# A convolution block on one core: thirteen slots instead of twelve, transfers by half slots, and four slots of one sample kept

## The chip, the cores and the metric

The kernel runs on one core of a Trainium2 chip. The time is the device time of one execution in microseconds (us). The kernel before takes 1641.06 us (median of three runs, 1640.28 to 1644.9).

## What is computed

x holds 16 samples of 64 x 64 pixels with 768 channels, in f32 (201.33 MB). Each sample is normalized in 32 groups of 24 channels, projected to 16 channels, and its mean decides the gates of four "experts": a 3 x 3 convolution after resizing by 1, 2, 4 and 8. The weighted sum is projected back to 768 channels and added to x.

```python
xc = conv2d(gn(x), conv1_w, conv1_b)                    # 768 -> 16, 1x1
pooled = mean(xc, (2, 3)); h = pooled @ H_w.T + H_b
g = softmax(where(top2(h), h, -inf))                    # 16 samples x 4 experts
experts = [down(conv2d(up(xc, 2**i), convl_w, convl_b)) for i in range(4)]
out = sum(stack(experts) * reshape(g, (4, 16, 1, 1, 1)))  # reshape, not transpose
return x + conv2d(out, conv2_w, conv2_b)                # 16 -> 768, 1x1
```

Because g is reshaped and not transposed, sample b is weighted with gates of the samples b//4, 4 + b//4, 8 + b//4 and 12 + b//4. So samples 0 to 3 need the means of samples 0, 4, 8 and 12; samples 4 to 7 those of 1, 5, 9 and 13; 8 to 11 those of 2, 6, 10 and 14; 12 to 15 those of 3, 7, 11 and 15.

## The kernel before, in words

A sample is 12.58 MB and on-chip memory holds twelve slots of 1.57 MB (128 partitions x 4 x 768 f32), an eighth of a sample each. Every sample passes twice. Stage A loads it (L), takes its statistics, transposes and projects it. Stage B comes after the gates of its quartet: it reloads the slots (R), adds the new values in place, and stores them (S). Only sample 15 is kept from A to B. So there are 128 loads, 120 reloads and 128 stores, 376 transfers of 1536 KB.

The order of work is written out in tables, one per engine, and each engine runs its table in order.

- SyncE runs TRANSFERS. `L4.3:3` loads slot 3 of sample 4 into place 3, `R0.4:1` reloads, `S0.0` stores, W1 and W2 are blocks of weight loads. A load waits until the place's former content has been transposed (stage A) or stored (stage B); a store waits for four adds. One transfer that waits holds all behind it.
- TensorE runs PE_ORDER: `T` transposes (24 a sample, L613), `M` projects (L626), `Z` sums the moments (L638), `G` and `H` do the gates (L657, L663), `C` is the convolution in seven parts (L678), `X` spreads the result (L695, L696), `E` projects back to 768 channels (32 tiles a sample, L707).
- ScalarE runs ACT_ORDER: `T` copies transposed data out of PSUM (L725), `S` takes 4 of 32 groups' statistics (L742, L744), `D` a square root, `I` and `H` copy results, `X` fills es4 (L778).
- VectorE runs DVE_ORDER: `B` is the statistics of 28 groups (L835), `F` turns them into scaled weights (L845 to L866), `V` and `W` prepare weights, `A` adds a tile to x in place (L915).
- GpSimd builds for each sample the weighted taps from four experts' tables (L560 to L564) and seven matrices "band" (L577), into BANDS = 4 buffers.

xT, the transposed data between ScalarE and TensorE, has XT = 4 buffers.

## Time and profile before

| what | value |
|---|---|
| median of the runs | 1641.06 us |
| the profiled execution | 1641.5 us |
| its span | 1639.8 us |
| PE, DVE, ACT, POOL busy | 1222.1, 1039.3, 657.6, 352.7 us |
| DMA moved | 593.46 MB, mean 362 GB/s |
| in the chain that ended last | DMA 45%, PE 28%, DVE 11%, SyncE's queue 7% |

The chain is followed back from the last instruction to what released each step. A transfer of 1536 KB takes long from issue to landing because several are queued; how far apart they follow one another is another number. Both can be read from the rows below.

### The profile page before, as it was taken

Reading aid. Unit: us, or ns where it says so; the run is one execution under the profiler, and the core shown is the slowest. Engines: PE = TensorE matmul, PEld = TensorE weight load, DVE = VectorE, ACT = ScalarE, POOL = GpSimd, SP = SyncE. Lnnn points to the kernel's source line nnn. Section 1 sums busy time; section 2 is a strip of 40 time slices with the busy share of each in tenths; the row PEclk is TensorE's granted clock in tenths of the full one; section 3 lists DMA queues with packets and bytes.
Section 4 is the critical chain, followed back from the end, with each engine's and each line's share of the span. In section 5 each row is a group of like instructions: output and inputs, shape, how many; then the busy total and the mean of one; then the engine's idle time right before and its main releaser. Section 6 shows DMA issues by size and latency. Waiting matters only on the chain.

```text
span 1639.8 us, 23721 instructions
## 1 busy us (share of the span) xinstructions
PE 1222.1 (75%) x8700; PEld 845.3 (52%) x8700; DVE 1039.3 (63%) x2763; ACT 657.6 (40%) x1549; POOL 352.7 (22%) x359
## 2 busy tenths in 40 slices
PE   1758879887889595949798968689597877766463
PEld 1636656655656363636565646366364544434231
DVE  7859765667576758555767575776845563453453
ACT  3758883444544453635454445435242100000000
POOL 2063008304010000052404100431004844211000
PEclk9889999989998797969889988799698887768555
DMA  9767774999999999957999999999999699999999
GB/s 359 270 230 273 280 298 157 397 350 406 367 406 397 409 398 409 393 222 289 400 343 392 379 408 378 406 335 410 410 402 403 237 403 411 415 413 415 414 414 381
DMA packets 203047, 593.46 MB, mean 362 GB/s; under 512 B 10290, under 2 KB 10290, under 8 KB 202932
## 3 DMA queue, kind: packets, MB, share of 16 engines
q1 hardware_dynamic: 202932, 591.95, 92.8%
q8 instruction: 69, 1.13, 0.3%
q14 instruction: 46, 0.38, 0.1%
HBM read 390.60 MB, written 201.33 MB: 361 GB/s over the span
## 4 chain that ended last, share of the span: by engine, by line
DMA 45%; PE 28%; DVE 11%; SPq 7%; issue 3%; ACT 2%; POOL 2%; DVEq 0%; ACTq 0%; POOLq 0%
DMA x_sb<-in_x 37%; PE ring_ps L613 11%; DMA out<-x_sb 8%; DVE x_sb L915 7%; PE img_ps L626 5%; SPq L427 5%; PE conv_ps L678 5%; PE ring_ps L707 5%; DVE stats L835 1%; POOL band L563 1%; PE ring_ps L695 1%; POOL taps L564 1%; ACT xT L725 1%; SPq L436 1%; PE ring_ps L638 1%
## 5 line engine op out<-in xcount | busy, mean ns | idle before, releaser
L915 DVE TENSOR_TENSOR x_sb<-x_sb,ring_ps 128x768 f32<-128x768 f32 x512 | 456.8, 949 | 358.1 <-PE ring_ps L707 188.4
L835 DVE BATCH_NORM_STATS2 stats<-x_sb 128x6 f32<-128x192 f32 x1792 | 472.5, 343 | 126.1 <-DMA x_sb<-in_x 68.5
L725 ACT COPY xT<-ring_ps 128x1024 f32<-128x1024 f32 x384 | 365.9, 1016 | 226.1 <-PE ring_ps L613 225.4
L613 PE MATMUL ring_ps<-ident,x_sb 128*128 128x128 f32 x3072 | 390.5, 285 | 72.7 <-DMA x_sb<-in_x 41.2
L707 PE MATMUL ring_ps<-w,es 128*128 128x512 f32 (+1 forms) x1024 | 322.6, 437 | 161.5 <-DVE x_sb L915 145.6
L613 PEld LDWEIGHTS ring_ps<-ident,x_sb 128*128 128x128 f32 x3072 | 354.5, 147 | 130.4 <-issue 88.6
L707 PEld LDWEIGHTS ring_ps<-w,es 128*128 128x128 f32 x1024 | 190.6, 229 | 275.2 <-DVE x_sb L915 152.3
L626 PE MATMUL img_ps<-xT,w 128*32 128x256 f32 x3072 | 219.9, 401 | 65.5 <-DVE w L866 55.0
L577 POOL TENSOR_TENSOR band<-taps,masks 128x640 f32<-128x640 f32 x112 | 169.7, 1541 | 444.0 <-PE conv_ps L678 442.8
L678 PE MATMUL conv_ps<-xc,band 128*128 128x1 f32 (+8 forms) x1120 | 219.9, 345 | 34.3 <-POOL band L577 20.5
L678 PEld LDWEIGHTS conv_ps<-xc,band 128*128 128x128 f32 x1120 | 156.1, 195 | 106.6 <-issue 93.4
L778 ACT CAST es<-ring_ps 64x1024 fp32r<-64x1024 f32 x64 | 63.5, 1004 | 363.5 <-PE ring_ps L696 363.3
L742 ACT ACTIVATE unread_squares<-x_sb 128x192 bf16<-128x192 f32 x256 | 93.6, 366 | 166.6 <-DMA x_sb<-in_x 127.8
L626 PEld LDWEIGHTS img_ps<-xT,w 128*32 128x32 f32 x3072 | 79.5, 111 | 149.1 <-DVE w L866 60.8
L560 POOL TENSOR_SCALAR taps<-experts,gates 128x400 f32<-128x400 f32 x16 | 20.6, 1285 | 590.7 <-DVE bias_es L900 585.7
L744 ACT ACTIVATE unread_copy<-x_sb 128x192 bf16<-128x192 f32 x256 | 89.7, 350 | 0.0
L695 PE MATMUL ring_ps<-es_hi,pick 128*64 128x512 f32 x128 | 64.2, 501 | 6.0 <-DVE bias_es L900 3.1
L563 POOL TENSOR_SCALAR band<-experts,gates 128x400 f32<-128x400 f32 x48 | 61.8, 1288 | 4.7
L696 PE MATMUL ring_ps<-es_lo,pick 128*64 128x512 f32 x128 | 61.2, 478 | 0.0
L638 PE MATMUL ring_ps<-stats,ones 128*128 128x192 f32 x128 | 35.1, 418 | 31.9 <-DVE stats L839 17.4
L564 POOL TENSOR_TENSOR taps<-taps,band 128x400 f32<-128x400 f32 x48 | 49.8, 1037 | 4.0
L742 ACT ACTIVATION_READ_ACCUMULATOR unread_squares<-x_sb 128x1 f32 x256 | 48.7, 190 | 0.0
(94 smaller groups left out, 341.8 us busy)
## 6 DMA issues: line engine op xcount, KB each, us to landing
x_sb<-in_x SPq DMA_DIRECT2D x248, 1536.0 KB, 18.5
out<-x_sb SPq DMA_DIRECT2D x128, 1536.0 KB, 12.9
w_rep<-in_L_conv_conv_w SPq DMA_DIRECT2D x8, 48.0 KB, 10.3
bias<-in_L_conv_conv_b SPq DMA_DIRECT2D x8, 0.1 KB, 10.0
wl_raw<-in_L_conv_convl_w SPq DMA_DIRECT2D x8, 9.0 KB, 7.0
bias_l<-in_L_conv_convl_b SPq DMA_DIRECT2D x8, 0.1 KB
gate_w<-in_L_conv_H_w SPq DMA_DIRECT2D x8, 0.2 KB
w_raw<-in_L_conv_conv_w SPq DMA_DIRECT2D x1, 48.0 KB
```

What stands on the lines that cost most here:

```text
L427: sp.dma_start(x_sb[:, n], x_v[s, i // 4, i % 4]).then_inc(loaded[n], 16)
L577: nc.gpsimd.tensor_tensor(band[:, n % BANDS], taps[:, MAT_ROW_TAP[m]].unsqueeze(2).broadcast_to(full), masks[:, MAT_MASK[m]].unsqueeze(1). ...
L613: last = nc.tensor.transpose(ring_ps[:, buf, q, half * P:(half + 1) * P], slot("L", a, 2 * c + half)[:, q, k * P:(k + 1) * P], ident[:, :])
L626: last = nc.tensor.matmul(img_ps[32 * q:32 * q + 32, 2 * P * (c % 2):2 * P * (c % 2 + 1)], w1[:, AI[a] % 2, k, c // 2, :], xT[:, at % XT, ...
L678: last = nc.tensor.matmul(conv_v[:, blk_out, col_out], band[:, n % BANDS, ax].rearrange("p h r -> p (h r)"), xc_v[:, XC_PLACE[b], blk_in, ...
L695: nc.tensor.matmul(into, high, es_hi[:, :], start=True, stop=False)
L707: last = nc.tensor.matmul(flat_ps[:, buf, part], es4[:, q, (i % 4) * P:(i % 4 + 1) * P], w2[:, part], start=True, stop=True)
L725: nc.scalar.copy(xT[:, at % XT], ring_ps[:, TURN["T", a, n] % RING]).then_inc(xT_copied, 1)
L742: nc.scalar.activation(unread_squares[:, :, :].rearrange("p (s q) c -> p s q c", s=2), group, ACT.Square, accum_out=stats[:, c, g, 0:1]).t ...
L744: nc.scalar.activation(unread_copy[:, :, :].rearrange("p (s q) c -> p s q c", s=2), group, ACT.Identity, scale=1.0 / HALF, accum_out=stats ...
L835: ins = nc.vector.bn_stats(stats[:, c, g, :], two_slots(n0, n1, g))
L915: nc.vector.tensor_tensor(x_sb[:, n, q, :], x_sb[:, n, q, :], flat_ps[:, TURN["E", b, t] % RING, 0:D], ALU.add).then_inc(added, 1)
```

## The change

Memory for a thirteenth slot comes from smaller buffers: XT goes from 4 to 3 and BANDS from 4 to 3; w1, pick, experts and masks shrink (expert 0 has only 3 x 3 taps that are not zero, and gets a table of its own; two of the five masks go, and the two matrices that used them are made by a memset and a product over one block). The spread (X) reads 32 of 128 rows of es_hi and es_lo.

Reloads and stores go by half slots of 768 KB, each half with its own semaphores; a half store waits for two adds. KEPT becomes {0: 4, 15: 8}: slots 0 to 3 of sample 0 stay on chip from A to B. There are 128 loads of 1536 KB, 232 reloads and 256 stores of 768 KB, 372 slots in all. The weights are loaded by ScalarE's queue, ahead of its first work. All four tables are written anew.

```diff
@@ -24,11 +24,11 @@
 CHUNKS = SPS // 2
 STEPS = CHUNKS * KB
 TILES = SPS * QN
-SLOTS = 12
+SLOTS = 13
 RING = 3
-XT = 4
+XT = 3
 XC = 6
-BANDS = 4
+BANDS = 3
 GV = G - 4
 HALF = 2 * QN * CG // 2
 GN_EPS = 1e-5
@@ -40,108 +40,138 @@
-KEPT = {15: 8}
+KEPT = {0: 4, 15: 8}
 TRANSFERS = """
-L4.0:0 L4.1:1 L4.2:2 W1 L4.3:3 L4.4:4 L4.5:5 L4.6:6 L4.7:7 L8.0:8 L8.1:9 L8.2:10 L8.3:11 L8.4:6 L8.5:7 L8.6:4 L8.7:5
+L4.0:0 L4.1:1 L4.2:2 L4.3:3 L4.4:4 L4.5:5 L4.6:6 L4.7:7 L8.0:8 L8.1:9 L8.2:10 L8.3:11 L8.4:12 L8.5:6 L8.6:7 L8.7:4
...
@@ -299,16 +341,17 @@
         x_sb = sb("x_sb", [P, SLOTS, QN, D])
         xT = sb("xT", [P, XT, QN, 2 * P])
         xc = sb("xc", [P, XC, PIX])
-        w1 = sb("w1", [P, 2, KB, 2, 2 * R])
+        w1 = sb("w1", [P, 2, KB, 3 * R])
         w1T = sb("w1T", [P, KB, R])
         stats = sb("stats", [P, CHUNKS, G, 6])
         ident = sb("ident", [P, P])
-        pick = sb("pick", [P, 2 * NH + 1, 2 * R], F32R)
+        pick = sb("pick", [P, 5, 2 * R], F32R)
         ones = sb("ones", [P, P])
         w2 = sb("w2", [P, D], F32R)
-        experts = sb("experts", [P, E, NT, NT, R])
+        experts = sb("experts", [P, E - 1, NT, NT, R])
+        expert_0 = sb("expert_0", [P, 3, 3, R])
         taps = sb("taps", [P, NT, NT, R])
-        masks = sb("masks", [P, 5, NH, R])
+        masks = sb("masks", [P, 3, NH, R])
         gates = sb("gates", [P, B, E])
         bias_es = sb("bias_es", [P, B])
         bias_l = sb("bias_l", [P, 1])
@@ -416,59 +459,42 @@
 
         @block.sync
         def _(sp):
-            def load(kind, s, i):
-                n, _, before = loads[kind, s, i]
-                if before is not None:
-                    was, s0, i0 = before
-                    if was == "L" and i0 >= KEPT.get(s0, 0):
-                        sp.wait_ge(transposed, AI[s0] * STEPS + (CHUNKS - i0 // 2) * KB)
+            stores = {half: 0 for half in stored}
+
+            def load(kind, s, i, place):
+                n, _, before = loads[(kind, s) + i]
+                for h, was in enumerate(before):
+                    if was is None:
+                        continue
+                    k0, s0, i0 = was[:3]
+                    half = (n[0], h) if kind == "L" else n
+                    if k0 == "L" and i0 >= KEPT.get(s0, 0):
+                        if h == 0:
+                            sp.wait_ge(transposed, AI[s0] * STEPS + (CHUNKS - i0 // 2) * KB)
                     else:
-                        sp.wait_ge(stored[n], 16 * stores[n])
-                sp.dma_start(x_sb[:, n], x_v[s, i // 4, i % 4]).then_inc(loaded[n], 16)
-
-            stores = [0] * SLOTS
-
-            def store(s, i):
-                kind = source[s, i]
-                n = loads[kind][0]
+                        sp.wait_ge(stored[half], 16 * stores[half])
+                if kind == "L":
+                    sp.dma_start(x_sb[:, n[0]], x_v[s, i[0] // 4, i[0] % 4]).then_inc(loaded[n], 16)
+                else:
+                    half = slice(2 * i[1], 2 * i[1] + 2)
+                    sp.dma_start(x_sb[:, n[0], 2 * n[1]:2 * n[1] + 2], x_v[s, i[0] // 4, i[0] % 4][:, half]
+                                 ).then_inc(loaded[n], 16)
+
+            def store(kind, s, i, place):
+                n = source[(s,) + i][1]
                 stores[n] += 1
-                sp.wait_ge(added, BI[s] * TILES + (i + 1) * QN)
-                sp.dma_start(out_v[s, i // 4, i % 4], x_sb[:, n]).then_inc(stored[n], 16)
-
...
+                sp.wait_ge(added, BI[s] * TILES + i[0] * QN + 2 * i[1] + 2)
+                sp.dma_start(out_v[s, i[0] // 4, i[0] % 4][:, 2 * i[1]:2 * i[1] + 2],
+                             x_sb[:, n[0], 2 * n[1]:2 * n[1] + 2]).then_inc(stored[n], 16)
+
+            for transfer in parse_transfers():
+                if transfer[0] == "S":
+                    store(*transfer)
                 else:
+                    load(*transfer)
+            for half in stored:
+                if stores[half]:
+                    sp.wait_ge(stored[half], 16 * stores[half])
@@ -554,14 +579,16 @@
 
                 flat = "p a x r -> p (a x r)"
                 all_e = taps[:, :, :, :].rearrange(flat)
-                for e in range(E):
-                    g, of_e = gates[:, b, e:e + 1], experts[:, e].rearrange(flat)
-                    if e == 0:
-                        link(nc.gpsimd.tensor_scalar(all_e, of_e, g, None, ALU.mult))
-                    else:
-                        part = band[:, NM * bi % BANDS].rearrange("p a h r -> p (a h r)")[:, 0:NT * NT * R]
-                        link(nc.gpsimd.tensor_scalar(part, of_e, g, None, ALU.mult))
-                        link(nc.gpsimd.tensor_tensor(all_e, all_e, part, ALU.add))
+                part = band[:, NM * bi % BANDS].rearrange("p a h r -> p (a h r)")
+                link(nc.gpsimd.tensor_scalar(all_e, experts[:, 0].rearrange(flat), gates[:, b, 1:2], None, ALU.mult))
+                for e in range(2, E):
+                    link(nc.gpsimd.tensor_scalar(part[:, 0:NT * NT * R], experts[:, e - 1].rearrange(flat),
+                                                 gates[:, b, e:e + 1], None, ALU.mult))
+                    link(nc.gpsimd.tensor_tensor(all_e, all_e, part[:, 0:NT * NT * R], ALU.add))
+                link(nc.gpsimd.tensor_scalar(part[:, 0:9 * R], expert_0[:, :, :, :].rearrange(flat), gates[:, b, 0:1],
+                                             None, ALU.mult))
+                link(nc.gpsimd.tensor_tensor(taps[:, 0:3, 0:3], taps[:, 0:3, 0:3],
+                                             part[:, 0:9 * R].rearrange("p (a x r) -> p a x r", a=3, x=3), ALU.add))
 
             for bi, b in enumerate(B_ORDER):
                 pool.wait_ge(gates_ready, b // 4 + 1)
@@ -573,9 +600,13 @@
                     n = NM * bi + part
                     if n >= BANDS and part:
                         pool.wait_ge(band_used, n - BANDS + 1)
-                    full = [P, NT, NH, R]
-                    nc.gpsimd.tensor_tensor(band[:, n % BANDS], taps[:, MAT_ROW_TAP[m]].unsqueeze(2).broadcast_to(full),
-                                            masks[:, MAT_MASK[m]].unsqueeze(1).broadcast_to(full),
+                    blocks = slice(0, 1) if m == TOP else slice(NH - 1, NH) if m == BOTTOM else slice(0, NH)
+                    if m in (TOP, BOTTOM):
+                        link(nc.gpsimd.memset(band[:, n % BANDS], 0.0))
+                    full = [P, NT, blocks.stop - blocks.start, R]
+                    nc.gpsimd.tensor_tensor(band[:, n % BANDS, :, blocks],
+                                            taps[:, MAT_ROW_TAP[m]].unsqueeze(2).broadcast_to(full),
+                                            masks[:, MAT_MASK[m], blocks].unsqueeze(1).broadcast_to(full),
                                             ALU.mult).then_inc(band_ready, 1)
 
         @block.tensor
@@ -690,10 +721,12 @@
                 for half in range(2):
                     h = 2 * (2 * (part % 2) + half) + part // 2
                     into = halves_ps[0:64, buf, half]
-                    high = pick[:, 2 * h + 1:2 * h + 3, :].rearrange("p n c -> p (n c)")
-                    low = pick[:, 2 * h:2 * h + 2, :].rearrange("p n c -> p (n c)")
-                    nc.tensor.matmul(into, high, es_hi[:, :], start=True, stop=False)
-                    last = nc.tensor.matmul(into, low, es_lo[:, :], start=False, stop=True)
+                    rows = slice(32 * (h // 2), 32 * (h // 2) + 32)
+                    first = 2 * (h % 2)
+                    high = pick[rows, first + 1:first + 3, :].rearrange("p n c -> p (n c)")
+                    low = pick[rows, first:first + 2, :].rearrange("p n c -> p (n c)")
+                    nc.tensor.matmul(into, high, es_hi[rows, :], start=True, stop=False)
+                    last = nc.tensor.matmul(into, low, es_lo[rows, :], start=False, stop=True)
                 last.then_inc(spread_done, 1)
 
             def tile(b, t):
@@ -715,6 +748,24 @@
 
         @block.scalar
         def _(act):
+            for h in range(NH):
+                rows = slice(R * h, R * h + R)
+                act.dma_start(w1_rep[rows, :], conv1_w.rearrange("r c y x -> r (c y x)")).then_inc(weights_in, 16)
+                act.dma_start(bias_1[rows, 0:1], conv1_b.unsqueeze(1)).then_inc(weights_in, 16)
...
+                act.dma_start(b2_raw[row:row + 1, :], conv2_b.unsqueeze(0)).then_inc(late_weights_in, 16)
             act.wait_ge(consts_ready, 1)
 
             def copy(a, n):
@@ -907,12 +959,12 @@
 
             def add(b, t):
                 i, q = divmod(t, QN)
-                kind = source[b, i]
-                n, count, _ = loads[kind]
-                if q == 0:
-                    dve.wait_ge(loaded[n], 16 * count)
+                load, (n, half) = source[b, i, q // 2]
+                place, count, _ = loads[load]
+                if q % 2 == 0:
+                    dve.wait_ge(loaded[place], 16 * count)
                 dve.wait_ge(expanded, BI[b] * TILES + t + 1)
-                nc.vector.tensor_tensor(x_sb[:, n, q, :], x_sb[:, n, q, :],
+                nc.vector.tensor_tensor(x_sb[:, n, 2 * half + q % 2, :], x_sb[:, n, 2 * half + q % 2, :],
                                         flat_ps[:, TURN["E", b, t] % RING, 0:D], ALU.add).then_inc(added, 1)
 
             program_of = {"B": groups, "F": fold, "L": low_half, "A": add, "P": softmax, "G": take_gates,
```

SyncE's queue at the start. Before: x_sb<-in_x are slots of x, the others are W1 and W2.

```order
1 L427 DMA x_sb<-in_x 128x4x768 x3
2 L441 DMA w_rep<-in_L_conv_conv_w 16x768
3 L442 DMA bias<-in_L_conv_conv_b 16x1
...
18 L427 DMA x_sb<-in_x 128x4x768 x13
19 L446 DMA wl_raw<-in_L_conv_convl_w 16x16x9 x8
20 L448 DMA w_raw<-in_L_conv_conv_w 128x6x16
...
38 L458 DMA b_raw<-in_L_conv_conv_b 1x768 x2
39 L427 DMA x_sb<-in_x 128x4x768 x32
40 L436 DMA out<-x_sb 128x4x768 x2
```

After:

```order
1 L477 DMA x_sb<-in_x 128x4x768 x41
2 L480 DMA x_sb<-in_x 128x2x768 x2
3 L477 DMA x_sb<-in_x 128x4x768 x3
4 L487 DMA out<-x_sb 128x2x768 x5
5 L480 DMA x_sb<-in_x 128x2x768
```

The 44 weight transfers are gone from SyncE's queue (they stand at the head of ScalarE's), and the first stores come after 45 slots' worth of loads, where 48 came before.

SyncE's queue between the last load of sample 5 and the first store of sample 5. Before, the third transfer of row 81 is L5.7, and row 90 begins with S5.0; 22 transfers lie from the one to the other, the store included.

```order
81 L427 DMA x_sb<-in_x 128x4x768 x5
82 L436 DMA out<-x_sb 128x4x768
83 L427 DMA x_sb<-in_x 128x4x768
84 L436 DMA out<-x_sb 128x4x768
85 L427 DMA x_sb<-in_x 128x4x768 x2
86 L436 DMA out<-x_sb 128x4x768
87 L427 DMA x_sb<-in_x 128x4x768 x2
88 L436 DMA out<-x_sb 128x4x768 x2
89 L427 DMA x_sb<-in_x 128x4x768 x9
90 L436 DMA out<-x_sb 128x4x768 x3
```

After, the last rows of the same stretch; it begins at row 89 (the first transfer there is L5.7), and row 121 begins with S5.0.0. From L5.7 to S5.0.0 it holds 27 slots' worth.

```order
109 L477 DMA x_sb<-in_x 128x4x768 x2
110 L487 DMA out<-x_sb 128x2x768
111 L477 DMA x_sb<-in_x 128x4x768
112 L487 DMA out<-x_sb 128x2x768
113 L480 DMA x_sb<-in_x 128x2x768
114 L477 DMA x_sb<-in_x 128x4x768
115 L487 DMA out<-x_sb 128x2x768
116 L480 DMA x_sb<-in_x 128x2x768 x2
117 L487 DMA out<-x_sb 128x2x768
118 L480 DMA x_sb<-in_x 128x2x768 x2
119 L487 DMA out<-x_sb 128x2x768 x2
120 L480 DMA x_sb<-in_x 128x2x768 x2
121 L487 DMA out<-x_sb 128x2x768 x3
```

Stores of sample 3 (rows 110 to 119) now stand right up to the first reloads and stores of sample 5, where nine loads in a row stood before. In the same way 33 transfers lay between L15.7 and S15.0 (the 256th and the 289th transfer), and 53.5 slots' worth lie there now (the 231st to the 284.5th).

GpSimd's work for one sample. Before, of 16 such blocks:

```order
183 L560 TENSOR_SCALAR taps<-experts,gates 128x400
184 L563 TENSOR_SCALAR band<-experts,gates 128x400
185 L564 TENSOR_TENSOR taps<-taps,band 128x400
186 L563 TENSOR_SCALAR band<-experts,gates 128x400
187 L564 TENSOR_TENSOR taps<-taps,band 128x400
188 L563 TENSOR_SCALAR band<-experts,gates 128x400
189 L564 TENSOR_TENSOR taps<-taps,band 128x400
190 L577 TENSOR_TENSOR band<-taps,masks 128x640 x7
```

After:

```order
259 L583 TENSOR_SCALAR taps<-experts,gates 128x400
260 L585 TENSOR_SCALAR band<-experts,gates 128x400
261 L587 TENSOR_TENSOR taps<-taps,band 128x400
262 L585 TENSOR_SCALAR band<-experts,gates 128x400
263 L587 TENSOR_TENSOR taps<-taps,band 128x400
264 L588 TENSOR_SCALAR band<-expert,gates 128x144
265 L590 TENSOR_TENSOR taps<-taps,band 128x3x48
266 L607 TENSOR_TENSOR band<-taps,masks 128x640 x5
267 L605 MEMSET band 128x640
268 L607 TENSOR_TENSOR band<-taps,masks 128x5x16
269 L605 MEMSET band 128x640
270 L607 TENSOR_TENSOR band<-taps,masks 128x5x16
```

One pair of passes over 400 elements is now over 144, and two of the seven products over 640 elements are a memset and a product over 80.

## Rows read from the trace of the kernel before

**Rows 1.** The page: DMA and GB/s over 40 slices, DMA queue, traffic of HBM.
```profile
DMA  9767774999999999957999999999999699999999
GB/s 359 270 230 273 280 298 157 397 350 406 367 406 397 409 398 409 393 222 289 400 343 392 379 408 378 406 335 410 410 402 403 237 403 411 415 413 415 414 414 381
q1 hardware_dynamic: 202932, 591.95, 92.8%
HBM read 390.60 MB, written 201.33 MB: 361 GB/s over the span
```

**Rows 2.** The DMA-issuing queue's waits: total us, times, longest.
```profile
SPq L436 <- DVE x_sb L915: 513.9, 121, 40.4
SPq L427 <- PE ring_ps L613: 300.7, 70, 23.4
SPq L427 <- DMA out<-x_sb: 178.1, 39, 14.9
```

**Rows 3.** Stretches: start:end, length, PE, PEld, DVE, ACT, POOL busy, clock, DMA, GB/s.
```profile
11.00:22.00 11.00, 1.51 (x6) 1.14 (x6) 7.66 (x30) 4.56 (x18) 0.00 (x0) 1.00 1.03 332
22.00:38.00 16.00, 0.28 (x2) 0.30 (x3) 15.97 (x64) 6.66 (x34) 0.00 (x0) 1.00 1.03 401
...
78.50:89.40 10.90, 10.90 (x117) 8.07 (x116) 7.61 (x29) 10.21 (x23) 0.00 (x0) 1.00 0.12 9
...
700.00:747.00 47.00, 28.69 (x164) 20.35 (x164) 25.27 (x96) 14.94 (x39) 31.45 (x24) 0.72 0.43 167
800.00:825.00 25.00, 16.37 (x85) 12.44 (x84) 16.23 (x52) 5.93 (x20) 14.75 (x12) 0.79 0.83 320
1070.00:1100.00 30.00, 22.84 (x164) 16.71 (x162) 23.76 (x44) 8.91 (x11) 13.02 (x10) 0.89 0.86 309
1267.00:1306.00 39.00, 32.55 (x167) 23.29 (x165) 18.21 (x22) 2.62 (x3) 29.78 (x23) 0.87 0.62 231
1330.00:1640.00 310.00, 185.62 (x613) 110.94 (x612) 145.06 (x164) 20.44 (x23) 50.17 (x37) 0.68 1.02 409
1628.00:1640.00 12.00, 0.00 (x0) 0.00 (x0) 0.00 (x0) 0.00 (x0) 0.00 (x0) 0.50 0.72 294
```

**Rows 4.** SyncE's issues at the start, in order of time: start us, us.
```profile
2.38 1.60 SPq L441 DMA_DIRECT2D w_rep<-in_L_conv_conv_w  x1
...
10.96 57.61 SPq L427 DMA_DIRECT2D x_sb<-in_x  x13
68.62 9.84 SPq L446 DMA_DIRECT2D wl_raw<-in_L_conv_convl_w  x8
...
89.45 188.09 SPq L427 DMA_DIRECT2D x_sb<-in_x  x32
280.81 3.84 SPq L436 DMA_DIRECT2D out<-x_sb  x2
```

**Rows 5.** VectorE in order of time at the start: start us, us.
```profile
21.94 7.37 DVE L835 BATCH_NORM_STATS2 stats<-x_sb 128x6 f32<-128x192 f32 x28 [3.06 <-DMA x_sb<-in_x]
...
49.94 0.35 DVE L852 RECIPROCAL norm<-norm 128x32 f32<-128x32 f32 x1 [2.12 <-ACT norm L729]
...
102.48 0.35 DVE L852 RECIPROCAL norm<-norm 128x32 f32<-128x32 f32 x1 [10.14 <-ACT norm L729]
...
114.36 0.96 DVE L814 CAST w_hi<-ring_ps 128x768 fp32r<-128x768 f32 x1 [2.96 <-PE ring_ps L651]
...
149.18 0.35 DVE L852 RECIPROCAL norm<-norm 128x32 f32<-128x32 f32 x1 [1.09 <-ACT norm L729]
192.32 0.35 DVE L852 RECIPROCAL norm<-norm 128x32 f32<-128x32 f32 x1 [0.85 <-ACT norm L729]
238.86 0.35 DVE L852 RECIPROCAL norm<-norm 128x32 f32<-128x32 f32 x1 [1.55 <-ACT norm L729]
```

**Rows 6.** SyncE's issues around the first store of sample 5.
```profile
612.40 19.56 SPq L427 DMA_DIRECT2D x_sb<-in_x  x5
...
672.58 34.38 SPq L427 DMA_DIRECT2D x_sb<-in_x  x9
747.34 7.29 SPq L436 DMA_DIRECT2D out<-x_sb  x3
```

**Rows 7.** SyncE's issues around the last samples' stores.
```profile
1126.89 26.74 SPq L427 DMA_DIRECT2D x_sb<-in_x  x7
...
1271.49 34.86 SPq L436 DMA_DIRECT2D out<-x_sb  x5
...
1507.24 10.92 SPq L427 DMA_DIRECT2D x_sb<-in_x  x3
...
1612.46 15.71 SPq L436 DMA_DIRECT2D out<-x_sb  x4
```

**Rows 8.** The page's DMA issues: KB each, us from issue to landing.
```profile
x_sb<-in_x SPq DMA_DIRECT2D x248, 1536.0 KB, 18.5
out<-x_sb SPq DMA_DIRECT2D x128, 1536.0 KB, 12.9
```

**Rows 9.** The page's groups of instructions that the smaller buffers touch.
```profile
L725 ACT COPY xT<-ring_ps 128x1024 f32<-128x1024 f32 x384 | 365.9, 1016 | 226.1 <-PE ring_ps L613 225.4
L577 POOL TENSOR_TENSOR band<-taps,masks 128x640 f32<-128x640 f32 x112 | 169.7, 1541 | 444.0 <-PE conv_ps L678 442.8
L678 PE MATMUL conv_ps<-xc,band 128*128 128x1 f32 (+8 forms) x1120 | 219.9, 345 | 34.3 <-POOL band L577 20.5
L563 POOL TENSOR_SCALAR band<-experts,gates 128x400 f32<-128x400 f32 x48 | 61.8, 1288 | 4.7
L564 POOL TENSOR_TENSOR taps<-taps,band 128x400 f32<-128x400 f32 x48 | 49.8, 1037 | 4.0
L695 PE MATMUL ring_ps<-es_hi,pick 128*64 128x512 f32 x128 | 64.2, 501 | 6.0 <-DVE bias_es L900 3.1
```

345 lines of the change are left out of this document (184 added, 161 removed).

## The prediction

> **What bounds the kernel now.** I read the page's slices first [rows 1]. All transfers go through one queue, its packets take 92.8% of sixteen engines' span, and in most slices the DMA digit is 9 with about 400 GB/s. The digits that are not 9 lie in two places: the first seven slices, where 157 to 298 GB/s are moved, and three dips, around slices 17 and 18, 26 and 31. So there are two regimes: near 400 GB/s only fewer bytes help, and in the holes something else is late. TensorE, busiest of the engines with 75% of the span, would leave 418 us, so it matters only where it stands in a chain.
>
> Next come the queue's waits [rows 2]: 513.9 us until VectorE's adds (stores), 300.7 until TensorE's transposes (loads of stage A), 178.1 until a store has landed (a place to become free). These are waits of the issuer, harmless while enough is queued: a load lands 18.5 us after its issue and a store 12.9 us [rows 8], while one slot at the 409 GB/s of 1330 to 1640 takes 1.573 MB / 409 = 3.85 us [rows 3]. About five slots are in flight. The stretches [rows 3] show where the cover is gone: 78.5 to 89.4 with 9 GB/s, 700 to 747 with 167, 1267 to 1306 with 231, and smaller ones at 800 (320) and 1070 (309).
>
> The first hole is explained by SyncE's own order [rows 4]. From 68.62 to 89.45 it issues the 28 transfers of W2, in 20.8 us, and the next load, of sample 12, is issued behind them. VectorE shows the price [rows 5]: its reciprocals of five samples stand at 49.94, 102.48, 149.18, 192.32 and 238.86, so periods of 52.5, 46.7, 43.1 and 46.5 us, and the long one contains a wait of 10.14 us for ScalarE's square root, which stands behind sample 12's statistics.
>
> The two large dips are the gates. S5.0 needs the gates of samples 1, 5, 9 and 13, thus all of A5. Its last load is the third of five issued from 612.40, the next stores of sample 5 come at 747.34, and after 672.58 nine loads end SyncE's work at 707 [rows 6]: every place is full and sample 3 is all stored. Similarly the last load of sample 15 is the fifth of seven issued from 1126.89, and after a wait five stores, among them the first of sample 15, take from 1271.49 to 1306.4 [rows 7].
>
> **The change, part by part.** The sum is made against the profiled execution, 1641.5 us (span 1639.8 and 1.7 around it), 0.4 above the median of 1641.06.
>
> *Weights on ScalarE's queue.* W1 goes from 2.38 to 10.96 on SyncE, with slot 4 of the first sample behind it, and VectorE waits 3.06 us for the second pair of slots [rows 4, 5]. Without W1, four slots at 409 GB/s are in at about 2 + 15.4 = 17.4 us, before VectorE is through with the first pair (18.9). So 3.1 us go. For W2, the wait of 10.14 goes, and of the next period (46.7 against 43.1, of which the wait of 2.96 for the weights' transposes is part, while VectorE's work on them stays) about 1: 11.1 us. The least is 0 (if another wait is just as late), the most 9.4 + 3.6 = 13. ScalarE now issues 44 transfers before its first statistics; at W1's pace (16 in 8.6 us) that is 23.6 us. It has sixteen groups to do before D4, four times half of the 6.66 us that two pairs of slots take in 22 to 38 [rows 3], and two copies (1016 ns [rows 9]), and would finish at 39, where VectorE's own part (four times 7.6 us from 11.2, and the weights' work) ends at about 43. This cover holds 4 us; beyond it each us counts fully.
>
> *GpSimd before the first store.* One of three added pairs of passes (1.288 + 1.037 us [rows 9]) is over 144 elements, not 400: if it goes by elements, 1.5 us, between nothing and 2.3. It is on the path once, before the first convolution. Later it is hidden behind other work. The first store waits for two adds instead of four, some 1.8 us, which I leave inside the other terms.
>
> *Slots kept and the thirteenth.* This is smaller than it looks. Four reloads vanish, 376 transfers become 372. But they vanish where the DMA had time: before the first store 48 loads were issued, now 45 slots' worth, as the kept slots occupy places. After it 328 were left (376 - 48), and now 327. One slot, 3.9 us.
>
> *Gates.* Here the thirteenth slot and the new tables count. Between L5.7 and S5.0 there were 22 transfers, 22 x 3.85 = 85 us, while the chain (statistics, projection, gates, matrices, convolution) took from a landing at about 640 to 747, 107 us. Now 27 slots' worth lie there, 104 us: 19 of the 26.8 us lost in 700 to 747 (0.57 of 47 [rows 3]) are covered. At sample 15 it is 33 against 53.5, which covers all of 0.38 x 39 = 14.8 us. The smaller holes at 800 and 1070 lose 4 us each, and I expect nothing there. Together 34 us at most; what was idle time of the DMA is no gain where the engines' own work is behind it, and it was at 70 to 83% for TensorE in these stretches. Nothing at all is the other end; nearer to the full cover, I take three quarters, 25 us.
>
> *Halves.* At the end the last store is half as long and waits for two adds: half a slot, 1.9 us, against a hole of 0.28 x 12 after 1628 = 3.4 us [rows 3]. There are 616 transfers instead of 376, 240 more. None of this size is in the trace. From above: in the stretch 11 to 22, where the 16 transfers of W1 pass in the queue, 332 GB/s were moved against 401 just after [rows 3]: 11 x (1 - 332/401) = 1.9 us, or 0.12 us each, so 29 us for 240. From below: nothing, and a gain is excluded since no byte is saved. Those weight transfers are of few and of tiny pieces, the halves of the same 3 KB pieces as before; I take 0.02 us, 5 in all, nearer to the row of the queue that is back-pressured at 10.92 us for three slots [rows 7], in which no gap can be seen.
>
> At this point a rule of the Trainium skill speaks against the change: "DMA: Bandwidth & Descriptors", on the anatomy of one DMA, gives a fixed cost of about 2.0 us per DMA (measured there for GpSimd's path) beside its bytes, most of it the wait for the last write to be confirmed. Were it paid one after another, the estimate by that page of the Trainium skill would be 240 x 2.0 = 480 us more. The row shows slots 3.6 us apart with 18.5 us from issue to landing, so by that rule, whose own account puts the cost into completion, the trace agrees: it lies in the latency and not in the spacing.
>
> *Smaller buffers.* ScalarE's copy takes 1016 ns and waits for TensorE, not the other way, in 225.4 us [rows 9]; with three buffers TensorE may transpose at most three ahead, and its tables do so. A band product takes 1541 ns, while a seventh of a convolution takes ten instructions, 219.9 us for 112 of them, so 1.96 us against 1.54. I cost both at nothing, hidden by DMA near 400 GB/s. If one band and one copy per sample came late it would be 16 x (1.54 + 1.02) = 41 us of TensorE; in the holes, a ninth of the span, that is 5 us. The cheaper last two of seven products can give back as much. The spread's matmuls (501 ns, 64.2 us in all) contract over 32 rows instead of 128: from nothing to half of that saved, off the path; I take nothing.
>
> Sum: 3.1 + 11.1 + 1.5 + 3.9 + 25 + 1.9 - 5 = 41.5, so 1600 us.
>
> **Rivals.**
>
> *Only the front and the bytes.* The dips stay since the rewritten tables put adds among stage A's work, and the same TensorE work has to be done before each gate. For it: TensorE is busy 0.83 of 1267 to 1306. Against it: only 0.61 of 700 to 747, where it waits for matrices and gates. Then 41.5 - 25 = 16.5, 1625 us.
>
> *DMA-bound from the first store on.* Between the 49th transfer at 280.8 and the 157th at 747.3, 4.32 us pass per transfer, and until the dip 3.96. If finer transfers and one more place bring all stretches to 3.85, 327 x 3.85 = 1259 us follow a first store at about 265, which is 1524; half of the way from 1600 to there is what I believe possible, since stage A is bound by its own work as at the start. About 1570 us.
>
> *The price of a transfer.* Each half costs the queue a fixed piece of time that cannot be overlapped. This is the mechanism on the other side: its place is every stretch near 400 GB/s, its price 240 times the piece, and from (41.5 + 5) / 240 = 0.19 us it makes the change slower than before. The row of W1 gives at most 0.12. At 0.12 it is 1600 + 24 = 1624, at 0.25 it is 1655. The Trainium skill's fixed cost per DMA ("DMA: Bandwidth & Descriptors", anatomy of one DMA) would be this mechanism if a tenth of it showed in the spacing.
>
> **How the numbers follow.** Forecast 1600 (its own range 1584 to 1616): 0.45. Front and bytes only, 1625: 0.23. DMA-bound, 1570: 0.17. Price of a transfer: 0.15, of which 0.10 above no change and 0.05 within it. No change is within 0.3% of 1641.06, thus 1636 to 1646. Of the second case 0.02 falls there. So faster 0.45 + 0.21 + 0.17 = 0.83, same 0.07, slower 0.10. The range of 1566 to 1636 leaves out most of the last case and a little of the third.
>
> **What would show it.** The gap of 10.14 us before a reciprocal gone and the first store near 265 (front). First store of sample 5 near 712 instead of 747 and over 300 GB/s before it; no stretch near 231 GB/s before the first stores of sample 8 (gates). 405 to 415 GB/s in the last 300 us with halves (price of a transfer: under 390 would make the third rival right). ScalarE's first statistics before 30 us. Wrong would be the forecast if the holes only moved, for instance to places where a half's wait holds SyncE's queue with less than five slots in flight.

## The result and the profile after

The changed kernel takes 1552.22 us (median of four runs, 1549.22 to 1555.05), the kernel before 1640.99 beside it: a ratio of 0.9454, interval 0.9431 to 0.9477. The gain is 88.8 us, where 41.5 were forecast. It lies outside the range, whose lower end was 1566. The profiled execution has a span of 1553.3 us.

The page's slices, main queue and traffic; they answer to [rows 1]:

```profile
DMA  9887845999999999999999999999999999999998
GB/s 327 315 305 275 304 155 199 411 409 395 380 410 410 410 409 390 410 345 394 407 408 409 397 400 362 411 415 415 415 415 413 383 405 413 414 412 410 415 413 333
q1 hardware_dynamic: 200320, 585.14, 96.0%
HBM read 384.30 MB, written 201.33 MB: 377 GB/s over the span
```

The first seven slices are still below 330 GB/s. Of the three dips one is left, shallower, at slice 17 (345; the first slice is 0, as in the prediction). Outside it 407 to 415 is what most slices show, where before 335 to 400 came up again and again. The queue's waits (total us, times, longest), against [rows 2]:

```profile
SPq L487 <- DVE x_sb L967: 291.7, 152, 6.4
SPq L477 <- PE ring_ps L644: 251.7, 67, 20.7
SPq L480 <- DMA out<-x_sb: 171.5, 68, 9.2
SPq L480 <- PE ring_ps L644: 38.2, 3, 35.3
```

Waiting for adds fell from 513.9 to 291.7 us, waiting for transposes only from 300.7 to 289.9 (251.7 in loads and 38.2 in reloads, one of these 35.3 long). Store waits have a longest of 6.4 us, where before one lasted 40.4.

To see where the 86.5 us between the two spans lie, I cut both executions at the same events: the first stores of samples 0, 3, 5, 4, 10 and 8, found by counting SyncE's issues against its list. Stretches of the kernel before (columns as in [rows 3], GB/s last):

```profile
280.80:585.40 304.60, 246.35 (x1883) 172.03 (x1884) 210.94 (x573) 142.16 (x339) 43.74 (x33) 0.89 1.00 390
585.40:747.30 161.90, 116.43 (x948) 82.17 (x945) 100.19 (x319) 79.78 (x191) 31.75 (x25) 0.84 0.85 332
747.30:1070.40 323.10, 264.56 (x1999) 187.06 (x2000) 218.73 (x622) 155.13 (x377) 64.24 (x48) 0.89 0.99 386
1070.40:1163.20 92.80, 75.10 (x575) 53.17 (x575) 65.08 (x151) 39.77 (x89) 17.18 (x13) 0.91 0.98 375
1163.20:1334.40 171.20, 141.03 (x839) 95.08 (x837) 101.60 (x165) 40.01 (x52) 67.49 (x51) 0.88 0.93 364
1334.40:1639.80 305.40, 181.71 (x590) 107.94 (x590) 141.28 (x160) 20.35 (x22) 45.93 (x34) 0.68 1.02 409
```

and of the changed one:

```profile
263.20:569.70 306.50, 256.92 (x2070) 180.18 (x2074) 228.94 (x656) 166.46 (x400) 41.22 (x40) 0.91 1.02 404
569.70:695.40 125.70, 97.01 (x759) 67.81 (x748) 92.63 (x288) 65.30 (x162) 27.16 (x26) 0.85 0.99 386
695.40:1027.10 331.70, 295.41 (x2434) 210.73 (x2434) 249.94 (x731) 192.68 (x454) 67.82 (x65) 0.94 1.02 398
1027.10:1087.50 60.40, 55.89 (x418) 38.88 (x419) 31.59 (x52) 22.69 (x25) 4.10 (x4) 0.89 1.03 415
1087.50:1245.90 158.40, 124.24 (x566) 78.67 (x564) 94.09 (x122) 19.50 (x23) 59.08 (x58) 0.78 1.02 407
1245.90:1553.30 307.40, 186.52 (x588) 104.98 (x586) 142.60 (x159) 20.41 (x22) 41.78 (x41) 0.60 1.00 402
```

In its best slices the kernel before moved 414 GB/s or so; at that rate a slot of 1.573 MB takes 3.80 us. What each stretch takes beyond 3.80 us for each of its slots I call its excess:

| from first store of | slots before, after | excess before, us | excess after, us | gained, us |
|---|---|---|---|---|
| start, to sample 0 | | 280.8 in all | 263.2 in all | 17.6 |
| 0 to 3 | 75, 79.5 | 19.6 | 4.4 | 15.2 |
| 3 to 5 (first gate) | 33, 28.5 | 36.6 | 17.4 | 19.2 |
| 5 to 4 | 80, 86 | 19.1 | 4.9 | 14.2 |
| 4 to 10 | 23, 16 | 5.4 | -0.4 | 5.8 |
| 10 to 8 (second gate) | 41, 41 | 15.4 | 2.6 | 12.8 |
| 8 to the end | 76, 76 | 16.6 | 18.6 | -2.0 |

With the one slot fewer (3.8) this is 86.6. So 17.6 us come at the front, 32.0 at the two gates, and 35.2 in the three stretches between, where the DMA digit was 9 before too. I call those the mixed stretches: stage A of one sample runs beside stage B of another.

How full the queue was there can be read from the same traces, by cutting them into pieces of 4 us and counting what was issued and had not landed. In the mixed stretches before, fewer than two slots were in flight for 84 us, and these pieces moved 290 GB/s; measured by bytes they hold 25 of 48 us of excess. With three slots or more in flight it was 401 GB/s for 533 us (17 us of excess), where the end of the kernel has 413. After, the pieces with fewer than two slots are 32 us at 343 GB/s (5.5 of 20 us), and with three or more it is 407 GB/s. So some 20 of the 28 us that this count shows as gained are time in which the queue had run short.

The first store of sample 5, against [rows 6] (start us, us):

```profile
682.85 4.19 SPq L487 DMA_DIRECT2D out<-x_sb  x2
688.50 2.22 SPq L480 DMA_DIRECT2D x_sb<-in_x  x2
695.37 3.83 SPq L487 DMA_DIRECT2D out<-x_sb  x3
```

It comes at 695.37 instead of 747.34, and SyncE issues reloads until 4.7 us ahead of it, where before it issued nothing for 40 us. ScalarE at the start:

```profile
9.10 8.47 ACTq L756 DMA_DIRECT2D wl_raw<-in_L_conv_convl_w  x8
...
18.11 9.33 ACTq L760 DMA_DIRECT2D gate_b<-in_L_conv_H_b  x1
...
35.40 0.79 ACTq L768 DMA_DIRECT2D b_raw<-in_L_conv_conv_b  x2
36.30 1.28 ACT L793 ACT_TABLE_LOAD   x1 [36.30 <-issue]
```

Its 44 weight transfers last until 36.2 us, and its first statistics follow at 36.30, where the prediction wanted them before 30. VectorE's first two pairs of slots, and the first step after its statistics of the first sample, which waits for TensorE's sums:

```profile
14.65 7.37 DVE L888 BATCH_NORM_STATS2 stats<-x_sb 128x6 f32<-128x192 f32 x28 [10.16 <-DMA x_sb<-in_x]
...
23.42 7.37 DVE L888 BATCH_NORM_STATS2 stats<-x_sb 128x6 f32<-128x192 f32 x28 [1.13 <-DMA x_sb<-in_x]
...
53.87 0.36 DVE L898 TENSOR_REDUCE small<-ring_ps 128x96 f32<-128x192 f32 x1 [4.48 <-PE ring_ps L669]
```

The same in the kernel before (its second pair is in [rows 5], at 21.94):

```profile
11.24 7.37 DVE L835 BATCH_NORM_STATS2 stats<-x_sb 128x6 f32<-128x192 f32 x28 [6.96 <-DMA x_sb<-in_x]
...
46.69 0.36 DVE L845 TENSOR_REDUCE small<-ring_ps 128x96 f32<-128x192 f32 x1 [0.69 <-PE ring_ps L638]
```

The first pair of slots is there 3.4 us later than before and the second 1.5 us later. VectorE's reciprocals of the first five samples, against [rows 5]:

```profile
56.86 0.35 DVE L905 RECIPROCAL norm<-norm 128x32 f32<-128x32 f32 x1 [1.76 <-ACT norm L780]
...
97.88 0.35 DVE L905 RECIPROCAL norm<-norm 128x32 f32<-128x32 f32 x1 [1.09 <-ACT norm L780]
...
141.97 0.35 DVE L905 RECIPROCAL norm<-norm 128x32 f32<-128x32 f32 x1 [1.09 <-ACT norm L780]
...
182.94 0.35 DVE L905 RECIPROCAL norm<-norm 128x32 f32<-128x32 f32 x1 [1.09 <-ACT norm L780]
...
223.21 0.35 DVE L905 RECIPROCAL norm<-norm 128x32 f32<-128x32 f32 x1 [0.40 <-ACT norm L780]
```

The first is 6.9 us later than before (49.94), the others 4.6, 7.2, 9.4 and 15.7 earlier. The wait of 10.14 is gone. The page's issues, against [rows 8], show that a half lands 14.4 us after its issue:

```profile
x_sb<-in_x SPq DMA_DIRECT2D x128, 1536.0 KB, 16.0
out<-x_sb SPq DMA_DIRECT2D x256, 768.0 KB, 14.4
x_sb<-in_x SPq DMA_DIRECT2D x232, 768.0 KB, 14.4
```

### The profile page after: what moved, and what is told of

Read it like the earlier page. It is cut to its first block, busy times and chain, and to the rows that moved or that the text cites. A ratio compares the mean times of both kernels' runs of the same rounds, so it can differ in the third digit from the quotient of the medians.

```text
span 1553.3 us, 24104 instructions
## 1 busy us (share of the span) xinstructions
PE 1208.5 (78%) x8700; PEld 827.1 (53%) x8700; DVE 1030.2 (66%) x2747; ACT 665.3 (43%) x1549; POOL 312.2 (20%) x381
## 4 chain that ended last, share of the span: by engine, by line
DMA 45%; PE 30%; SPq 9%; DVE 8%; ACT 2%; ACTq 2%; issue 2%; POOL 1%; DVEq 0%
DMA x_sb<-in_x 32%; PE ring_ps L644 13%; DMA out<-x_sb 13%; PE img_ps L657 6%; PE conv_ps L709 6%; DVE x_sb L967 5%; SPq L480 5%; SPq L487 4%; PE ring_ps L740 3%; DVE stats L888 1%; ACT unread_squares L793 1%; ACT unread_copy L795 1%; ACTq L760 1%; ACTq L756 1%; SPq L477 1%
## 5 line engine op out<-in xcount | busy, mean ns | idle before, releaser
L776 ACT COPY xT<-ring_ps 128x1024 f32<-128x1024 f32 x384 | 375.8, 1014 | 263.5 <-PE ring_ps L644 233.2
L644 PE MATMUL ring_ps<-ident,x_sb 128*128 128x128 f32 x3072 | 401.1, 289 | 65.0 <-DMA x_sb<-in_x 41.3
L740 PE MATMUL ring_ps<-w,es 128*128 128x512 f32 (+1 forms) x1024 | 337.5, 446 | 145.2 <-DVE x_sb L967 140.4
L644 PEld LDWEIGHTS ring_ps<-ident,x_sb 128*128 128x128 f32 x3072 | 361.1, 149 | 128.6 <-issue 97.2
L709 PE MATMUL conv_ps<-xc,band 128*128 128x1 f32 (+8 forms) x1120 | 227.5, 351 | 19.2 <-POOL band L607 10.3
L607 POOL TENSOR_TENSOR band<-taps,masks 128x640 f32<-128x640 f32 (+1 forms) x112 | 133.0, 1202 | 530.9 <-PE conv_ps L709 527.1
L793 ACT ACTIVATION_READ_ACCUMULATOR unread_squares<-x_sb 128x1 f32 x256 | 48.7, 190 | 0.0
L795 ACT ACTIVATION_READ_ACCUMULATOR unread_copy<-x_sb 128x1 f32 x256 | 48.5, 189 | 0.0
L728 PE MATMUL ring_ps<-es_hi,pick 32*64 32x512 f32 x128 | 33.1, 530 | 13.4 <-DVE x_sb L967 12.0
L585 POOL TENSOR_SCALAR band<-experts,gates 128x400 f32<-128x400 f32 x32 | 41.2, 1286 | 3.1
L669 PEld LDWEIGHTS ring_ps<-stats,ones 128*128 128x128 f32 x128 | 23.5, 218 | 31.8 <-DVE stats L892 23.3
## 6 DMA issues: line engine op xcount, KB each, us to landing
out<-x_sb SPq DMA_DIRECT2D x256, 768.0 KB, 14.4
x_sb<-in_x SPq DMA_DIRECT2D x232, 768.0 KB, 14.4
```

Source lines behind the costliest of these rows:

```text
L607: nc.gpsimd.tensor_tensor(band[:, n % BANDS, :, blocks], taps[:, MAT_ROW_TAP[m]].unsqueeze(2).broadcast_to(full), masks[:, MAT_MASK[m], bl ...
L644: last = nc.tensor.transpose(ring_ps[:, buf, q, half * P:(half + 1) * P], slot("L", a, 2 * c + half)[:, q, k * P:(k + 1) * P], ident[:, :])
L709: last = nc.tensor.matmul(conv_v[:, blk_out, col_out], band[:, n % BANDS, ax].rearrange("p h r -> p (h r)"), xc_v[:, XC_PLACE[b], blk_in, ...
L740: last = nc.tensor.matmul(flat_ps[:, buf, part], es4[:, q, (i % 4) * P:(i % 4 + 1) * P], w2[:, part], start=True, stop=True)
L776: nc.scalar.copy(xT[:, at % XT], ring_ps[:, TURN["T", a, n] % RING]).then_inc(xT_copied, 1)
L793: nc.scalar.activation(unread_squares[:, :, :].rearrange("p (s q) c -> p s q c", s=2), group, ACT.Square, accum_out=stats[:, c, g, 0:1]).t ...
```

## The experiments

All ratios are against the kernel before on the same chip.

### The changed kernel with one part undone

**Whole transfers, same orders.** The two words of a half pair are merged where the second stood.

```diff
-L2.4:11 S0.5.0 S0.5.1 L2.5:2 S0.6.0 S0.6.1 L2.6:3 R0.7.0:8.0 R0.7.1:8.1 L2.7:6 R1.0.0:0.0 R1.0.1:0.1 L3.0:4 S0.7.0
+R0.5:12 S0.3 R0.6:10 S0.4 L2.4:11 S0.5 L2.5:2 S0.6 L2.6:3 R0.7:8 L2.7:6 R1.0:0 L3.0:4 L3.1:12 S0.7 L3.2:10 S1.0 R1.1:8
...
-                sp.wait_ge(added, BI[s] * TILES + i[0] * QN + 2 * i[1] + 2)
+                sp.wait_ge(added, BI[s] * TILES + (i[0] + 1) * QN)
```

> The changed kernel with reloads and stores of whole slots (1536 KB), each at the place in SyncE's order where its second half stood, everything else as changed. Theory 1 (the 63 us of holes went because of the thirteenth place and the new order; halves only shorten the tail): 1555 to 1565 us. Rival (halves did it: a place turns over sooner since half a store and half a reload can start after two adds): 1585 to 1615 us, with holes at the gates and less than 400 GB/s between 330 and 1000 us.

Measured: 1719.88 us, 1.0485 (1.0466 to 1.0505), 168 us above the changed kernel. The queue's waits:

```profile
SPq L455 <- DVE x_sb L934: 697.7, 121, 24.0
SPq L449 <- PE ring_ps L611: 483.9, 73, 32.4
```

The waits for adds went from 291.7 to 697.7 us. This is far above both expectations (1555 to 1565 and 1585 to 1615): the order cannot do without halves as it stands; whether another list of transfers would let it is tried below.

**Weights back on SyncE's queue**, W1 behind the third load and W2 behind L8.7 as before.

```diff
-L4.0:0 L4.1:1 L4.2:2 L4.3:3 L4.4:4 L4.5:5 L4.6:6 L4.7:7 L8.0:8 L8.1:9 L8.2:10 L8.3:11 L8.4:12 L8.5:6 L8.6:7 L8.7:4
+L4.0:0 L4.1:1 L4.2:2 W1 L4.3:3 L4.4:4 L4.5:5 L4.6:6 L4.7:7 L8.0:8 L8.1:9 L8.2:10 L8.3:11 L8.4:12 L8.5:6 L8.6:7 L8.7:4
...
-                act.dma_start(w1_rep[rows, :], conv1_w.rearrange("r c y x -> r (c y x)")).then_inc(weights_in, 16)
+                    sp.dma_start(w1_rep[rows, :], conv1_w.rearrange("r c y x -> r (c y x)")).then_inc(weights_in, 16)
```

> The changed kernel with the weights back on SyncE's queue, W1 behind the third slot and W2 behind the last load of sample 8. If the front's 17.6 us come from the weights, as forecast: first store 10 to 17 us later, 1562 to 1570 us. Rival, that the weights on ScalarE cost as much as they save (its first fold is 6.9 us later than before): within 3 us of 1552.

Measured: 1552.83 us, 0.9467 (0.9453 to 0.9482): the move is worth nothing here. VectorE's first two reciprocals:

```profile
49.93 0.35 DVE L916 RECIPROCAL norm<-norm 128x32 f32<-128x32 f32 x1 [2.02 <-ACT norm L791]
...
98.02 0.35 DVE L916 RECIPROCAL norm<-norm 128x32 f32<-128x32 f32 x1 [7.45 <-ACT norm L791]
```

The first comes 6.9 us sooner than in the changed kernel, the second at the same time, behind a wait of 7.45. What the one queue gains the other gives back.

**Sample 0's slots not kept** (four more reloads ahead of the first store).

```diff
-KEPT = {0: 4, 15: 8}
+KEPT = {15: 8}
-L0.7:1 L1.0:4 L1.1:0 L1.2:3 L1.3:2 L1.4:5 L1.5:1 L1.6:7 L1.7:6 L2.0:9 R0.4.0:6.0 R0.4.1:6.1 L2.1:7 L2.2:1 L2.3:5
+L0.7:1 L1.0:4 L1.1:0 L1.2:3 L1.3:2 L1.4:5 L1.5:1 L1.6:7 L1.7:6 L2.0:9 R0.0.0:12.0 R0.0.1:12.1 R0.1.0:10.0 R0.1.1:10.1
+R0.2.0:11.0 R0.2.1:11.1 R0.3.0:8.0 R0.3.1:8.1 R0.4.0:6.0 R0.4.1:6.1 L2.1:7 L2.2:1 L2.3:5 S0.0.0 S0.0.1 S0.1.0 S0.1.1
```

> The changed kernel with slots 0 to 3 of sample 0 not kept: eight half reloads are issued into the same places just ahead of R0.4.0, where the queue had 125 GB/s to move. As forecast, the 6.3 MB are free there: 1552 to 1556 us. Rival, that bytes count at the full rate: 4 x 3.85 = 15 us, 1567 us.

Measured: 1551.34 us, 0.9455 (0.9439 to 0.947). Nothing either, as expected: the four reloads fit into DMA time that is idle before the first store, which comes at 264.1 us against 263.2.

### The old order with parts of the change

**Old orders and twelve places, with halves, the smaller buffers and the weights on ScalarE.** The three engines' tables are those of the kernel before, and its transfers stand with each R and S cut in two. Against the changed kernel:

```diff
-SLOTS = 13
+SLOTS = 12
-KEPT = {0: 4, 15: 8}
+KEPT = {15: 8}
```

> The changed code with the tables of before (order of all engines, twelve places, only sample 15 kept), reloads and stores cut in halves at the same place, XT and BANDS 3, weights on ScalarE. It has all of the change but the order, the thirteenth place and the kept slots. Theory 1: only the front's gain, 1620 to 1632 us. Rival (halves): 1575 to 1600 us.

Measured: 1621.88 us, 0.9888 (0.9872 to 0.9904), inside the first expectation. The number does not bear out the reason given for it, though: two later runs split these 18.6 us, and the larger part is the halves', not the front's. **Only the weights and the memory-saving code** (tables, cheaper passes, narrow spread), XT and BANDS still 4, whole transfers, against the kernel before:

```diff
-L4.0:0 L4.1:1 L4.2:2 W1 L4.3:3 L4.4:4 L4.5:5 L4.6:6 L4.7:7 L8.0:8 L8.1:9 L8.2:10 L8.3:11 L8.4:6 L8.5:7 L8.6:4 L8.7:5
+L4.0:0 L4.1:1 L4.2:2 L4.3:3 L4.4:4 L4.5:5 L4.6:6 L4.7:7 L8.0:8 L8.1:9 L8.2:10 L8.3:11 L8.4:6 L8.5:7 L8.6:4 L8.7:5
...
+                act.dma_start(w1_rep[rows, :], conv1_w.rearrange("r c y x -> r (c y x)")).then_inc(weights_in, 16)
```

> The old order, twelve places, whole transfers, XT and BANDS at 4 as before; the weights go by ScalarE's queue, and the shrunk tables, the cheaper GpSimd passes and the narrow spread are in. By the sum of the prediction: 14.2 for the weights and 1.5 for GpSimd, 1625 us. Rival: as inside the changed kernel ScalarE's 36 us of issuing give back what SyncE's queue gains, 1638 to 1643.

Measured: 1632.64 us, 0.9948 (0.9931 to 0.9965), so 8.5 us: between the two expectations. Its first two reciprocals:

```profile
57.16 0.35 DVE L862 RECIPROCAL norm<-norm 128x32 f32<-128x32 f32 x1 [1.79 <-ACT norm L737]
...
100.49 0.35 DVE L862 RECIPROCAL norm<-norm 128x32 f32<-128x32 f32 x1 [0.86 <-ACT norm L737]
```

7.2 us later than before in the first, 2.0 sooner in the second; the first store comes at 276.4 instead of 280.8. **The same with XT and BANDS at 3:**

```diff
-XT = 4
+XT = 3
-BANDS = 4
+BANDS = 3
```

> As the one before, with XT and BANDS at 3. By the prediction the smaller buffers cost nothing: the same as the one before within 3 us. Against the fourth experiment (the same with halves, 1621.9) it gives what halves are worth in the old order: by the orders drawn up anew 18 us, so 1640; by the prediction (tail 1.9, price 5) nothing, so 1622.

Measured: 1635.11 us, 0.9964 (0.9945 to 0.9983). That is 2.5 us more than with the larger buffers, within the intervals nothing; and against the two numbers for halves, 1640 and 1622, it lies nearer to the first. By the ratios halves are worth 12.5 us in the old order (0.9888 against 0.9964), with 4 us of uncertainty on either side. Two stretches of this kernel, from the first store to sample 3's, and the last 76 slots:

```profile
276.10:580.00 303.90, 248.46 (x1883) 172.45 (x1884) 210.06 (x570) 144.05 (x339) 39.33 (x39) 0.88 1.00 390
1327.80:1632.20 304.40, 181.74 (x590) 103.75 (x590) 141.17 (x160) 20.00 (x22) 42.71 (x41) 0.62 1.02 409
```

The same two of the one with halves, with the same order:

```profile
275.60:575.00 299.40, 245.19 (x1879) 170.15 (x1882) 208.94 (x571) 143.77 (x338) 41.21 (x40) 0.89 1.02 399
1316.60:1620.30 303.70, 184.09 (x584) 103.82 (x584) 141.75 (x158) 20.41 (x22) 40.55 (x40) 0.60 1.01 407
```

In the mixed stretch halves raise the rate from 390 to 399 GB/s. In the last stretch the 152 halves take 303.7 us and the 76 wholes took 304.4: **a transfer more has no price that can be seen** (-0.7 us for 76 more). The last store, half as long, is in that difference; if it saved the 1.9 us of the prediction, 1.2 us are left for the price, 0.016 us a transfer.

### Orders drawn up by me

I drew up all four tables by a plain rule: each engine takes what is ready first, by durations read from the traces, and SyncE chooses between load, reload and store by a few fixed preferences. First a set with durations that turned out too short. One line of SyncE's list of the first of them against the kernel before (all four tables are replaced; the other three have the changed kernel's code with SLOTS 12 or 13, halves or wholes):

```diff
-L0.7:5 L1.0:0 L1.1:1 L1.2:2 L1.3:3 L1.4:4 L1.5:5 L1.6:6 L1.7:7 L2.0:8 L2.1:9 L2.2:10 L2.3:11 R0.0:6 R0.1:7 L2.4:4
+L0.7:5 L1.0:0 L1.1:1 L1.2:2 L1.3:3 L1.4:4 L1.5:5 L1.6:6 L1.7:7 L2.0:8 L2.1:9 R0.0:10 R0.1:11 R0.2:6 L2.2:7 L2.3:4
```

> The kernel before with nothing changed but its four tables: twelve places, whole slots, XT and BANDS 4, weights on SyncE, only sample 15 kept. The tables are drawn up anew, each engine taking among its streams of work what is ready first by the durations of the trace. Theory 2, formed after e1 to e4 (the holes go when adds and transfers are spread over the gates; places and halves only have to fit the order): 1535 to 1570 us. Rival (the thirteenth place is needed): above 1600. Rival (halves are needed): above 1600.

> The changed code with twelve places, only sample 15 kept, halves, and tables by the same rules as in e5. Theory 2: within 15 us of e5. If halves are what counts: 40 us or more below e5. If the thirteenth place counts: above 1600 us like e5.

> The changed code with thirteen places, four slots of sample 0 kept, whole slots, and tables by the same rules as in e5. Theory 2: within 15 us of e5, thus 150 us below e1, which has the same places and whole slots in an order made for halves. If halves are what counts: above 1600 us. If the thirteenth place counts: 40 us or more below e5.

> Everything of the change (thirteen places, halves, four slots of sample 0 kept) with tables by the same rules as in e5. Theory 2: the lowest of the four, 1530 to 1560 us, and no more than 20 us below e5. It also tells how far the changed kernel's own tables are from what these rules give.

Measured: 1655.0, 1655.83, 1643.82 and 1656.48 us (1.0088, 1.0094, 1.0017, 1.0099, each with 0.0015 to 0.0024 on either side). They lie within 13 us, and none is faster than the kernel before: the theory, which had 1535 to 1570 for the first and 1530 to 1560 for the last, failed. With these poor orders halves do not help, and only the one with thirteen places and wholes stands apart, 11 us below the first. The durations were then fitted to the ten executions known by that time, and the tables drawn up again; each has the code of its like among the four before. SyncE's list around sample 5's first store, with twelve places and wholes, against the kernel before:

```diff
-R5.1:9 R5.2:10 S5.0 S5.1 S5.2 L7.1:2 L7.2:6 R5.3:1 R5.4:9 L7.3:10 L7.4:0 L7.5:4 L7.6:5 S5.3 S5.4 L7.7:8 L14.0:3 R5.5:7
+R5.1:6 L7.0:5 L7.1:7 L7.2:2 L7.3:1 L7.4:10 L7.5:0 L7.6:3 L7.7:9 S3.7 R5.2:11 S5.0 R5.3:8 S5.1 R5.4:4 S5.2 R5.5:6 S5.3
```

> The kernel before with its four tables drawn up anew and nothing else (twelve slots, whole transfers, weights on SyncE's queue, sample 15 alone kept, old buffers). The tables are planned by taking on each engine what is ready first, with durations fitted to the traces of the ten kernels run so far; that of the second to the fifth experiment of the orders were not fitted. Theory (the order of the work closes most of the holes, a place and halves add little): 1580 us, 1565 to 1600. Rival 1 (halves are what lets reloads and stage A share the places): 1620 or more. Rival 2 (the thirteenth place decides): 1620 or more here and in the next one as well.

> The changed kernel's code and buffers with twelve slots, half transfers, weights on ScalarE's queue, sample 15 alone kept, and tables drawn up as in the one before. Theory (order): 1565 us, so 15 below it. Rival 1 (halves): 1565 too, but then with 50 us or more to the two with whole slots. Rival 2 (thirteenth place): 1620 or more.

> The changed kernel's code and buffers with thirteen slots, four of sample 0 kept, but whole transfers, and tables drawn up in the same way. Theory (order): 1580 us. Rival 1 (halves): 1620 or more. Rival 2 (thirteenth place): 1565 to 1580 while those with twelve are at 1620.

> The changed kernel with its own code, places and halves, and tables drawn up in the same way instead of its own. Theory (order): 1563 us, within 15 us of the changed kernel and of the one with twelve slots and halves. Rival (its gain rests on something that these plans do not hold, such as where its reloads stand): 1590 or more.

Measured: 1621.53 us (0.9873, 0.9847 to 0.9899), 1603.88 (0.9772, 0.9755 to 0.9789), 1618.71 (0.9858, 0.9837 to 0.9879) and 1600.94 (0.9755, 0.9734 to 0.9776). All came out 38 to 42 us above the theory's numbers: in level the theory failed, and those with wholes stand at the 1620 of the first rival. The new order alone, in the code of the kernel before, is worth 19.2 us (1640.71 beside it; about 4 us of uncertainty on either side). With halves the time is 17.7 and 17.8 us less than with wholes, with the thirteenth place 2.8 and 2.9 less than with twelve. But each of the four has tables of its own, and the first alone has the old buffers and the weights on SyncE's queue; so these are differences between whole plans, and not prices of one part with the rest held fixed. The rates of the first of them in 40 slices:

```profile
GB/s 359 277 174 302 311 302 281 152 342 411 408 406 403 395 411 408 392 394 374 409 409 400 407 414 405 411 377 406 112 397 415 404 354 415 415 416 417 417 417 390
```

And of the last:

```profile
GB/s 329 224 290 296 270 226 168 187 404 407 394 402 386 411 396 396 410 401 409 363 410 402 411 393 411 361 412 300 337 413 413 386 397 415 416 416 416 416 416 384
```

They keep low rates until slice 8 (down to 152 and 168), have their first stores at 343.1 and 311.8 instead of 263.2, and a hole is left near the second gate (112; 300). The last has the changed kernel's code to the letter, so the 48.7 us between the two are the order's alone. Its first store comes 48.6 us later, but behind 49 slots of loads instead of 45; so part of that time (four slots, 15.2 us) is work that the changed kernel has yet to do.

### The changed kernel's engines, other transfers

TensorE, ScalarE and VectorE keep the changed kernel's tables. Only SyncE's list is drawn up anew, by one rule for all four. A line of it with 13 places and halves; with 12 places SLOTS is 12; wholes have the code of the first experiment, but are listed anew and not merged; KEPT is {15: 8} in all but the first:

```diff
-L2.4:11 S0.5.0 S0.5.1 L2.5:2 S0.6.0 S0.6.1 L2.6:3 R0.7.0:8.0 R0.7.1:8.1 L2.7:6 R1.0.0:0.0 R1.0.1:0.1 L3.0:4 S0.7.0
+R0.6.1:11.1 R0.7.0:8.0 S0.5.0 L2.5:2 L2.6:3 R0.7.1:8.1 S0.5.1 R1.0.0:12.0 R1.0.1:12.1 S0.6.0 S0.6.1 L2.7:0 L3.0:4
```

> The changed kernel with its own orders of TensorE, ScalarE and VectorE, and only SyncE's list of transfers drawn up anew for thirteen places and halves. It says what such a list costs against the kernel's own. All theories: within 15 us of the changed kernel, 1555 to 1567.

> As the one before, with twelve places (sample 15 alone kept). Theory (the order of the engines closes the holes; the place is worth 3 us as in the pair of orders of mine, up to 12 here since this order is tighter): 1560 to 1578. Rival (the thirteenth place is what lets stage A run past the gates): 1600 or more.

> As the first of these, with whole transfers for reloads and stores (sample 15 alone kept; the four slots of sample 0 were worth nothing), listed anew and not merely merged as in the first experiment, which lost 167 us. Theory (order; halves worth 10 to 18 us): 1570 to 1582. Rival (this order lives from the halves): 1620 or more, as merging them suggests.

> As the first of these, with twelve places and whole transfers. If place and halves stand in for one another (either gives stage A the room that this order wants), this one falls far behind the other two: my durations give 1690. If they only add up, 1590.

Measured: 1573.79 us (0.9585, 0.9569 to 0.9601), 1604.09 (0.9772, 0.9752 to 0.9791), 1583.67 (0.9648, 0.9633 to 0.9664), 1739.38 (1.0596, 1.058 to 1.0612). The stretch from the first store to sample 3's, in the first:

```profile
263.00:580.50 317.50, 258.73 (x2042) 181.15 (x2042) 228.95 (x655) 164.75 (x398) 41.17 (x40) 0.90 1.01 391
```

With twelve places and halves:

```profile
270.70:598.80 328.10, 260.83 (x2034) 183.01 (x2027) 228.68 (x652) 162.80 (x389) 39.52 (x39) 0.87 0.98 377
```

With thirteen and wholes:

```profile
266.70:602.60 335.90, 273.02 (x2178) 191.82 (x2178) 236.46 (x682) 174.40 (x414) 39.46 (x39) 0.88 0.99 383
```

With twelve and wholes:

```profile
269.60:673.80 404.20, 288.25 (x2178) 204.96 (x2178) 235.55 (x682) 174.94 (x414) 39.55 (x39) 0.82 0.86 323
```

391, 377, 383 and 323 GB/s, against the 404 of the changed kernel. With either the place or halves the new engines' order is faster than the kernel before; without both, with the list that my rule gives, it is 98.6 us slower. With my lists the place is worth 30.3 us beside halves, and halves 9.9 beside the place; with the kernel's own list another 21.6 are gained. The first expectation (1555 to 1567) was missed by 7 us, the second is past the theory's 1578 and at the rival's 1600, so the place matters more in this order than in mine, the third is 2 us past its range, and the fourth shows the two standing in for one another, stronger than the 1690 had it.

### The runs by kind of stretch

Excess over 3.80 us for each slot, summed as above, in us:

| kernel | first store | mixed stretches | gates | last 76 |
|---|---|---|---|---|
| before | 280.8 | 44.1 | 52.0 | 16.6 |
| old order, weights moved | 276.4 | 42.7 | 49.6 | 15.4 |
| same, smaller buffers | 276.1 | 40.7 | 53.4 | 15.6 |
| same, halves | 275.6 | 29.5 | 53.9 | 14.9 |
| new engines, my list: 12, halves | 270.7 | 41.3 | 30.3 | 12.3 |
| 13, wholes | 266.7 | 43.1 | 17.2 | 13.3 |
| 13, halves | 263.0 | 30.1 | 25.4 | 16.7 |
| 12, wholes | 269.6 | 164.2 | 45.6 | 11.7 |
| changed kernel | 263.2 | 8.9 | 20.0 | 18.6 |
| same, wholes merged in | 263.5 | 144.5 | 48.7 | 18.0 |
| my orders, refitted: 12, wholes | 343.1 | 19.4 | 42.7 | 4.1 |
| 12, halves | 316.5 | 37.2 | 5.6 | 11.6 |
| 13, wholes | 317.2 | 34.2 | 21.5 | 13.3 |
| 13, halves | 311.8 | 45.2 | 8.6 | 5.5 |

The gates follow the order of the work: 50 to 54 in the old one, with halves or without, and 17 to 30 with the new engines' order, with twelve places or thirteen, as long as it has the place or the halves. The clearest pair is the one with twelve places and halves in the same code: 53.9 in the old order, 30.3 in the new (SyncE's list differs too).

Within one order of the engines the mixed stretches follow the room. In the old order halves take 11 us out of them. In the new one the place does so beside halves (41.3 to 30.1), and halves beside the place (43.1 to 30.1). The kernel's own list then takes them from 30.1 to 8.9: with code, places and engines' tables the same, 21.2 us lie there, of the 24.5 between the two profiled spans (21.6 between the medians). From one order to another the rule does not hold, as the last four rows show: there twelve places with wholes have the least in the mixed stretches, after the latest first store.

## Why the prediction was wrong, point by point

**Front, right in size at the first store, wrong in its reason.** 15.7 us of terms and an uncounted 1.8 were forecast, and 17.6 came. But the weights' move, 14.2 us of it, is worth 8.5 us together with the cheaper passes and the rest of the memory-saving code in the old order (4.4 at the first store), and nothing in the changed kernel. One step that failed is that ScalarE "would finish at 39" with its statistics and hide. Its issuing took 36.2 us instead of 23.6, since the eight pieces of wl_raw took 8.47 us and gate_b alone 9.33. The forecast had named the cover of 4 us beyond which each us counts. It had taken W1's pace for W2 as well, although its own [rows 4] have 20.8 us for the 28 transfers of W2, of which wl_raw took 9.84; by them the issuing would have been 29.4 us. The other is the 3.1 us for W1: the first slots landed later and not sooner, the first pair by 3.4 us and the second by 1.5. The two together make the first sample's fold 6.9 us late: VectorE's own part ends 3.4 us later, and its wait for TensorE's sums, which wait for ScalarE's statistics, grows from 0.69 to 4.48 us. The other 13 us at the first store come with the new engines' order and the place (270.7 with twelve, 263.0 with thirteen).

**One slot fewer.** 3.9 us in the sum, and 3.8 in the account. Yet with the four slots reloaded before the first store the time is the same, since those reloads are free; the fewer slots afterwards come from the order, not from keeping.

**Gates, right.** 34 us were the most, 25 were taken, 32.0 came: 19.2 at the first, where 19 had been worked out as covered, and 12.8 of 14.8 at the second. In passing, the forecast says that TensorE was at 70 to 83% in these stretches, but its own row has 0.61 in 700 to 747. The first store of sample 5 was forecast near 712 and came at 695.4, because the first mixed stretch gave 15.2 us that were not in the sum. Over 300 GB/s before it: 386.

**The step that failed: "The smaller holes at 800 and 1070 lose 4 us each, and I expect nothing there", and before it "near 400 GB/s only fewer bytes help".** The stretches between the gates ran at 375 to 390 GB/s and not at 414. In a row of slices these are digits of 9 with 335 to 400 between them, easy to pass over; summed over 178 slots they were 44.1 us of excess, nearly as much as the gates' 52.0. The forecast read its losses off the DMA's busy share, and that was 1.00 where 390 GB/s were moved. More than half of the excess were short holes like the gates', in which fewer than two slots were in flight. The change took 35.2 of the 44.1 us, most of it out of these. Why 401 GB/s and not 413 were moved even with three or more in flight, no run shows. The rival "DMA-bound from the first store on" had the mechanism and its full size (1524), but went half of the way, for the reason that stage A is bound by its own work; in the mixed stretches it was not: TensorE was busy 0.81, 0.82 and 0.81 of the three before, and 0.84, 0.89 and 0.93 after.

**Halves, wrong in sign.** The sum took 5 us of cost and 1.9 of gain at the tail. The price in the spacing is too small to be seen (303.7 us with 152 halves, 304.4 with 76 wholes). The tail cannot be told apart: the last stretch went from 305.4 to 307.4, but it is 306.8 with wholes merged in. The gain I left out is in the mixed stretches: the whole kernel gains 12.5 us by halves in the old order and 9.9 with thirteen places in the new engines' order. My reading is that a half place can be stored and loaded again while the other half is still waiting for adds. From the issue of a reload to the landing of its store, for reloads between 330 and 980 us, 36.2 us passed on average in the old order with wholes and 33.4 with halves, and in the changed kernel's order 35.5 with wholes merged in and 29.1 with halves. (The kernel before has 36.9, with 2.54 places held for stage B at a time; the changed one holds 1.96.) No run separates this from the other thing that halves do: a store that waits for two adds holds SyncE's queue for less time (waits for adds 524.0 us with wholes in the old order, 357.5 with halves). I looked at what the transfer costs and not at what it holds. The Trainium skill ("DMA: Bandwidth & Descriptors", anatomy of one DMA) has a fixed cost per DMA of about 2.0 us, measured for GpSimd's path and mostly completion latency. The experiment agrees in that nothing like it shows in the spacing: at 768 KB the rate was 407 GB/s, against 409 at 1536 KB. The same page of the Trainium skill has, under its heading on bandwidth, the rule to batch to at least 1 MiB for 75% of the peak; these transfers are below that and show no loss. Several of them are in flight at a time (14.4 us from issue to landing, at 1.9 for each half), which may be why; no run here has them one by one.

**Smaller buffers.** Costed at nothing, and 2.5 us in the old order, which the intervals do not tell from nothing.

**The total.** Front 17.6 (forecast 15.7), slot 3.8 (3.9), gates 32.0 (25), mixed stretches 35.2 (0), tail and price -2.0 (-3.1). Of the 45.0 us that the sum was short of the 86.5 between the spans, three quarters are the mixed stretches.

What stays open: the mechanism of the last 21.6 us, between my list and the kernel's own with the same engines. The traces show one difference: by my list 45.6 us pass from a reload's issue to the landing of its store and 2.97 places are held for stage B, by the kernel's own 29.1 us and 1.96. That would mean that my list reloads too early and keeps a place from stage A, but no run changes this alone. Open is also whether a better order for twelve places exists than those tried (1603.9 and 1604.1 with halves, 1621.5 without). No version tried beats the changed kernel by more than the noise; the one that keeps nothing of sample 0 equals it at 1551.34.

## What to carry to other kernels

Where one queue bounds a kernel, compute the time per piece in every stretch against the best stretch of the same trace, and sum the difference; a digit of 9 hides 2 to 9%, and such stretches together can weigh as much as two visible dips (here 44.1 us against 52.0). Ask of a finer transfer first how much sooner it gives its buffer back, and only then what it costs. An order of work is fitted to its buffers: with one rule for SyncE's list, the new engines' order gained 67 us with thirteen places and halves and lost 98.6 with twelve and wholes, so a part of such a change is not to be priced by taking it away from the whole alone.

## What the runs showed of the hardware

- A store or load of 768 KB behind others moves bytes as fast as one of 1536 KB: 407 against 409 GB/s over 300 us, in the same order.
- Issues on ScalarE's queue beside a full queue of SyncE: w_rep took 0.44 to 0.52 us each, but the eight of wl_raw 8.47 us and the one of gate_b 9.33, 36 us for all 44. On SyncE's queue before, wl_raw took 9.84 us and gate_b 0.54, and the last 28 together 20.8. The first slots of x landed 3.4 us later beside them. The Trainium skill ("DMA: Bandwidth & Descriptors", issuing engines are not separate DMA queues) has it that a second issuing engine saves only the time on the sequencer. The trace agrees, and adds that here the second sequencer needed 7 us more than the first for the same transfers (36.2 against 8.6 + 20.8). With the weights on either queue the changed kernel takes the same time (1552.83 and 1552.22 us).
